# A one-core graph layer: tile widths of the last strips, one root, one comparison, and who makes the gate logits

## The chip, the cores and the metric

The kernel runs on one core of a Trainium2 chip. TensorE multiplies, VectorE, ScalarE and GpSimd (POOL) do elementwise work, and SyncE (SP) issues most DMAs. The metric is the device time of one execution in microseconds. The kernel before was timed three times: median 1168.58, from 1165.75 to 1169.1. One further execution was profiled.

## The reference

There are N = 3125 nodes with D = 256 features and E = 53125 weighted edges (src, dst), sorted by dst. In short:

```
xn = layernorm(x)
A[d, s] = sum of edge_weight over the edges s -> d      (3125 x 3125)
h  = A xn                                               (N x 256)
s0 = softmax((A h) W0^T + b0)                           (N x 128)
s1 = softmax((A [s0]) W1^T + b1)                        (N x 128)
gnn = tanh([s0, s1] + h)
mix = linear attention of xn: q, k, v projections, layernorm per head, k^T v, output projection
x1 = x + gnn + mix
probs = softmax(layernorm(x1) gate_w + gate_b)          (8 experts)
each token goes to its best expert if its place there is below the capacity of 489
out = x1 + (relu(token w1 + b1) w2 + b2) * prob
```

The reference runs four equal heads and averages them, and W1 enters as a 128 x 128 matrix.

## The kernel before

**Tiles, strips and units.** Nodes lie in 25 tiles of 128 (NT); the last tile holds 53 (LAST). The matrix A is built densely, one block of 128 sources by 128 destinations at a time. A strip is a group of destination tiles (STRIPS): six strips of four tiles (512 columns), and tile 24 alone (128 columns, of which 53 are nodes). A unit is one source tile j of one strip, so four blocks; the last strip has seven units of up to four source tiles. That makes 157 units (UNITS).

**The loop over units.** Every engine walks the same iterations, written out by hand with offsets. In iteration `it`, VectorE makes the one-hot operands of unit it-2 (`hots`, L1037 to L1046: source compared with a ramp, destination compared with a ramp, and, from unit 25 on, the source block times the edge weight). They lie in four buffers (`hot`). For the first 25 units (LEAD) ScalarE weighs them (`weigh`, L742). TensorE builds unit it-3 into one of two PSUM banks (`build`, L1491; an own-tile block, L1493, is added on the diagonal), ScalarE evicts it into the ring (`evac`, L752) and stores a chunk of five units to DRAM (`adj_dram`), and TensorE applies unit it-4 to xn (`apply`, L1508, last strip L1510), which accumulates h. At the end of a strip its h is copied out (`strip_out`), then every node tile is turned and multiplied by W0 (`hidden_node`, evicted by `hn_out`). The attention's products (`mix`, `mixed`) are placed in the loop at MIX_AT. The first 25 iterations also load and rank the edges (`spread`, `slot`, `ranks`, `slots`); the edge windows are loaded by SyncE one by one (L441 to L443). Four groups of windows are prepared on VectorE (`prepare`).

**The start.** ScalarE copies constants, waits for the centred k and v weights from TensorE and copies them (L687), and then takes the square root of the variances (`roots`, L698), on which the normalisation waits.

**The two z layers.** A is read back from DRAM, chunk by chunk, into a ring of five slots (L548). SyncE issues a load when the slot's old chunk is freed; the third load (slot 0) waits until the last unit is applied and all stores have landed. `strip(l, k)` multiplies by it (L1658), and other work is put between its 25 source tiles as inserts: `turns` (L1412 in layer 0, L1674 in layer 1), and in layer 1 also `gate_turn`, `logits` (L1694) and `counts` (L1703 to L1711). The second layer has its own strips (Z1): five of four tiles, then [20, 21], [22, 23] and [24]. [20, 21] and [22, 23] read the same five chunks.

**Gating.** After a strip of the second layer VectorE adds the bias (L1231), takes the maximum, normalises after ScalarE's exponentials, finishes x1 (L1247), takes moments (L1252, L1255) and an inverse root by iteration (`root`), places the group before (`slotted`), writes the normalised tokens (L1303), and for the first two tiles of each of four groups (DOTS = 4, DOT_TILES = 2) makes the eight gate logits itself, one fused multiply and sum each (`dots`, L1327). For the other tiles TensorE transposes x1 (`gate_turn`), ScalarE copies it (`xtout`) and TensorE multiplies by the gate (`logits`). `chosen` adds the bias and picks the expert; TensorE's `counts` waits for it. POOL scatters the tokens to DRAM. When all are there they are loaded back, and eight experts follow (L1746, L1758). Tiles 22 to 24 are one gating group.

A second path for inputs with too many edges per block (`more_rounds`) is not taken with these inputs.

Of the kernel before, what the change touches and what calls it, by code (L numbers as in the profile page):

```python
# [16 lines left out]
D = 256  # L17
# [46 lines left out]
DOTS, DOT_TILES = 4, 2  # L64
# [16 lines left out]

def chunk_of(u):
    return u // 5


def last_unit(n):
    return min(5 * n + 4, NU - 1)

# [8 lines left out]
for _t in range(NT - 1):  # L97
    _k, _i = _t // 4, _t % 4
    HN_AT[NT * _k + 30 + (5 * _i if _k < 5 else _i)] = _t
# [10 lines left out]
def graph_program(nc, a, out):  # L110
    ctx = ExitStack()
    with ctx:
# [320 lines left out]
        def _(sp):  # L433
# [42 lines left out]
            with more_rounds(sp):  # L476
# [11 lines left out]
                def put(c, jj, last):  # L488
# [4 lines left out]
                    to = adj_dram[31, :, jj * P:(jj + 1) * P] if last else adj_dram[30][:, ds(c * 5 * P + jj * P, P)]  # L493
                    sp.dma_start(to, e_tile[:, 6 * 512:NP]).then_inc(m_store, 16)
                    sp.wait_ge(m_store, j * 32 + 32)
                    sp.sem_inc(m_kept, 1)
                with sp.Fori(0, 4) as c:
                    for jj in range(5):
                        put(c, jj, False)
                for jj in range(5):  # L500
                    put(4, jj, True)
# [5 lines left out]
                sp.dma_start(e_chunk, adj_dram[30]).then_inc(m_chunk, 16)  # L507
                sp.wait_ge(m_app, 32)
                sp.dma_start(e_chunk[:, 0:5 * P], adj_dram[31, :, 0:5 * P]).then_inc(m_chunk, 16)
# [22 lines left out]
            for l in (0, 1):  # L532
                for q in range(NC):
# [13 lines left out]
                    w = 5 * 512 if q < NC - 1 else 5 * P  # L547
# [125 lines left out]
        def _(act):  # L673
# [71 lines left out]
            def evac(u):  # L745
                n = chunk_of(u)
                w = len(UNITS[u]) * P
                if u % 5 == 0 and n >= 2:
# [3 lines left out]
                nc.scalar.copy(RING[:, n % 2, u % 5 * 512:u % 5 * 512 + w], ps[:, u % 2, 0:w]).then_inc(s_bev, 1)  # L752
                if u == last_unit(n):
                    act.wait_ge(s_bev, u + 1)
                    w = 5 * 512 if n < NC - 1 else 5 * P
                    act.dma_start(adj_dram[n, :, 0:w], RING[:, n % 2, 0:w]).then_inc(s_ast[n % 2], 16)

            def strip_out(k):
                w = len(STRIPS[k]) * P
# [4 lines left out]
            roots(0)  # L764
            for j in range(3):
                normal(j)
# [30 lines left out]
            def zout(l, k):  # L797
                w = len((STRIPS, Z1)[l][k]) * P
# [20 lines left out]
            def xtout(k):  # L819
# [6 lines left out]
                for b in range(i0 // 2, (i0 + n + 1) // 2):  # L826
                    w = min(2, i0 + n - 2 * b)
                    last = nc.scalar.copy(xtb[g % 2][:, 2 * b:2 * b + w, :], ps[:, XTB + b, 0:w * D].rearrange("p (t n) -> p t n", n=D))
# [55 lines left out]
        def _(dve):  # L884
# [138 lines left out]
            def hots(u):  # L1023
# [7 lines left out]
                if u < NT * (NS - 1):  # L1031
                    field = lambda f: recs[:, f, j * NR + s:j * NR + s + n]
                else:
                    field = lambda f: recs[:, f, :].rearrange("p (t g) -> p t g", g=NR)[:, j:j + n, s]
                grid = lambda f: field(f).unsqueeze(2).to_broadcast([P, n, P])
                every = iota_n[:, :].unsqueeze(1).to_broadcast([P, n, P])
                v.tensor_tensor(h[:, 0, 0:n, :], every, grid(0), ALU.is_equal).then_inc(s_eq, 1)  # L1037
# [5 lines left out]
                last = v.tensor_tensor(h[:, 1, 0:n, :], every, grid(1), ALU.is_equal)  # L1043
                if u >= LEAD:
                    dve.wait_ge(s_eq, u + 1)
                    last = v.tensor_tensor(h[:, 0, 0:n, :], h[:, 0, 0:n, :], grid(2), ALU.mult)  # L1046
                last.then_inc(s_hot, 1)

            def strip_out(k):
                w = len(STRIPS[k]) * P  # L1050
# [113 lines left out]
            mixed(NT - 3)  # L1164
            hn_out(NT - 1)
# [622 lines left out]
```

## Time and profile before

| | |
|---|---|
| median of three executions | 1168.58 us |
| lowest and highest | 1165.75 and 1169.1 us |
| the profiled execution | 1178.36 us |
| its span | 1176.6 us |
| mean granted TensorE clock | 0.973 |
| TensorE busy | 1109.7 us (94%) |
| VectorE busy | 738.8 us (63%) |
| ScalarE busy | 315.3 us (27%) |

The span is the time from the first to the last recorded instruction, in one profiled execution. Busy time of TensorE is modelled from the starts of its instructions; an engine that isn't the bound may idle at no cost. The stages by time: up to about 226 us edges are ranked while the graph is built; from there to 622 the graph is built and applied; 626 to 767 is the first z layer; 767 to about 937 the second layer with the gating; 937 to the end the experts.

### The profile page before, as it was taken

To read this page: it belongs to the slowest core of one execution; us is meant where nothing else is said; L and a number is where in the kernel's file an instruction comes from. 1 tells how busy PE (TensorE), PEld (TensorE's weight loads), DVE (VectorE), ACT (ScalarE), POOL (GpSimd) and SP (SyncE) were. 2 spreads that over 40 slices of the span, in tenths; PEclk is the share of its full clock that TensorE was granted. 3 is DMA by queue.
4 is the path that set the end of the run, shared out by engine and by line. 5 is a ranking of instruction groups with operands and counts; after the bars stand their busy time and mean duration, and the time that the engine had idled before them with its cause. 6 is when DMAs were issued, how large, how long until landed. Compare 5 with 4: busy or idle time off the path is not lost.

```text
span 1176.6 us, 14070 instructions
## 1 busy us (share of the span) xinstructions
PE 1109.7 (94%) x4819; PEld 697.4 (59%) x4819; DVE 738.8 (63%) x1688; ACT 315.3 (27%) x1031; POOL 167.6 (14%) x206
## 2 busy tenths in 40 slices
PE   4879989999999999999998999999999699999995
PEld 2546666666666666666684444544448556666664
DVE  7989989998786977768740111116787425555444
ACT  4557767411212212112220110102112211112220
POOL 1013222301010100010000000000244421111111
PEclk8799989999999999999998999999999799999998
DMA  6110111123323333332228988797994475555620
GB/s 170 14 30 27 46 45 46 45 90 125 127 115 136 116 118 120 119 147 107 90 96 319 337 334 298 273 345 276 312 325 169 144 212 123 118 126 140 141 70 7
DMA packets 78869, 176.43 MB, mean 150 GB/s; under 512 B 33583, under 2 KB 62026, under 8 KB 66638
## 3 DMA queue, kind: packets, MB, share of 16 engines
q1 hardware_dynamic: 67550, 124.81, 33.3%
q10 hardware_dynamic: 7120, 42.67, 9.0%
q0 software_dynamic: 4128, 8.04, 2.0%
q8 instruction: 41, 0.67, 0.2%
q14 instruction: 30, 0.25, 0.1%
HBM read 114.87 MB, written 63.09 MB: 151 GB/s over the span
## 4 chain that ended last, share of the span: by engine, by line
PE 81%; DVE 8%; SPq 4%; issue 3%; ACT 2%; another core or an unknown queue 1%; DMA 0%; POOL 0%; POOLq 0%; DVEq 0%; ACTq 0%
PE ps L1508 20%; PE ps L1658 19%; PE ps L1491 11%; PE ps L1758 9%; PE ps L1746 9%; SPq L443 2%; PE ps L1534 2%; PE ps L1475 2%; PE ps L1461 1%; PE ps L1412 1%; PE ps L1761 1%; PE ps L1510 1%; DVE W L997 1%; SPq L441 1%
## 5 line engine op out<-in xcount | busy, mean ns | idle before, releaser
L1658 PE MATMUL ps<-RING,RY 128*128 128x512 f32 (+2 forms) x750 | 279.8, 531 | 4.4 <-issue 4.4
L1508 PE MATMUL ps<-RING,XX 128*128 128x512 f32 x600 | 282.6, 593 | 0.3 <-ACT RING L752 0.3
L1658 PEld LDWEIGHTS ps<-RING,RY 128*128 128x128 f32 x750 | 136.4, 196 | 131.0 <-issue 128.8
L1491 PEld LDWEIGHTS ps<-RING 128*128 128x128 f32 x1250 | 163.6, 193 | 45.8 <-issue 44.7
L752 ACT COPY RING<-ps 128x512 f32<-128x512 f32 (+1 forms) x157 | 91.8, 585 | 315.4 <-PE ps L1491 299.5
L1491 PE MATMUL ps<-RING 128*128 128x128 f32 x1250 | 170.8, 278 | 0.5 <-ACT RING L742 0.5
L1508 PEld LDWEIGHTS ps<-RING,XX 128*128 128x128 f32 x600 | 102.7, 191 | 72.9 <-issue 71.7
L1037 DVE TENSOR_TENSOR RING<-iota_n,RY 128x512 f32<-128x512 f32 (+1 forms) x157 | 108.1, 689 | 42.0 <-PE ps L1491 38.8
L1043 DVE TENSOR_TENSOR RING<-iota_n,RY 128x512 f32<-128x512 f32 (+1 forms) x157 | 117.4, 748 | 0.0
L1046 DVE TENSOR_TENSOR RING<-RING,RY 128x512 f32<-128x512 f32 x132 | 90.3, 684 | 0.0
L875 ACT ACTIVATE RY<-ps,b1T 128x489 f32<-128x489 f32 x64 | 42.9, 671 | 171.8 <-PE ps L1746 170.8
L1385 DVE SCALAR_TENSOR_TENSOR W<-ps,RING,W 128x256 f32<-128x256 f32 (+1 forms) x32 | 15.5, 484 | 98.8 <-PE ps L1758 97.8
L1216 DVE TENSOR_REDUCE nmx<-ps 128x4 f32<-128x512 f32 (+1 forms) x7 | 4.4, 635 | 113.6 <-PE ps L1412 113.6
L645 POOL DMA_INDIRECT xbuf_dram<-XX,sidx x25 | 25.1, 1002 | 341.4 <-DVE sidx L1315 335.9
L631 POOL TENSOR_TENSOR XX<-XX,bo_b 128x256 f32<-128x256 f32 x25 | 29.3, 1174 | 255.0 <-PE ps L1491 254.9
L668 POOL DMA_INDIRECT out<-W,RING x32 | 31.5, 985 | 188.9 <-DVE W L1392 152.0
L1758 PE MATMUL ps<-XT,RY 128*128 128x256 f32 (+1 forms) x256 | 55.9, 379 | 0.0
L1758 PE MATMUL ps<-RING,RY 128*128 128x256 f32 (+1 forms) x256 | 55.9, 379 | 0.0
L1475 PE MATMUL ps<-wkvT,XT 128*128 128x512 f32 x100 | 52.5, 651 | 3.5 <-ACT XT L715 3.5
L1746 PE MATMUL ps<-RING,XT 128*128 128x489 f32 x128 | 53.2, 574 | 0.0
L1746 PE MATMUL ps<-RING 128*128 128x489 f32 x128 | 53.1, 573 | 0.0
L1758 PEld LDWEIGHTS ps<-RING,RY 128*128 128x128 f32 (+1 forms) x256 | 47.4, 185 | 9.3 <-issue 1.8
(255 smaller groups left out, 1286.7 us busy)
## 6 DMA issues: line engine op xcount, KB each, us to landing
RING<-adj_dram SPq DMA_DIRECT2D x62, 1280.0 KB
adj_dram<-RING ACTq DMA_DIRECT2D x31, 1280.0 KB, 4.5
rbuf_dram<-W SPq DMA_DIRECT2D x8, 516.0 KB, 5.3
RING<-rbuf_dram SPq DMA_DIRECT2D x8, 516.0 KB, 4.1
xbuf_dram<-W SPq DMA_DIRECT2D x8, 512.0 KB, 3.3
XT<-in_L_ffn_w SPq DMA_DIRECT2D x16, 256.0 KB
XT<-in_L_ffn_w SPq DMA_DIRECT2D x4, 1024.0 KB
RING<-in_L_ffn_w SPq DMA_DIRECT2D x16, 256.0 KB
```

The source lines that it names most:

```text
L668: gp.indirect_dma_start(out[:, :], bass.IndirectOffsetOnAxis(ap=rbs[0:n, e % 2, c, D + 1:RES].bitcast(I32), axis=0), ybs[0:n, e % 2, c, :] ...
L752: nc.scalar.copy(RING[:, n % 2, u % 5 * 512:u % 5 * 512 + w], ps[:, u % 2, 0:w]).then_inc(s_bev, 1)
L875: nc.scalar.activation(hmT[:, f, 0:CAPX], ps[:, 2 + f % 3, 0:CAPX], ACT.Relu, bias=b1T[:, f, e:e + 1]).then_inc(s_hidv, 1)
L1037: v.tensor_tensor(h[:, 0, 0:n, :], every, grid(0), ALU.is_equal).then_inc(s_eq, 1)
L1043: last = v.tensor_tensor(h[:, 1, 0:n, :], every, grid(1), ALU.is_equal)
L1046: last = v.tensor_tensor(h[:, 0, 0:n, :], h[:, 0, 0:n, :], grid(2), ALU.mult)
L1475: last = nc.tensor.matmul(ps[:, PROD, :], XT[:, c, m * P:(m + 1) * P], wkvT[:, c, :], start=(c == 0), stop=(c == 1))
L1491: last = nc.tensor.matmul(o[:, i * P:(i + 1) * P], h[:, 0, i, :], h[:, 1, i, :], start=True, stop=(j != s))
L1508: last = nc.tensor.matmul(ps[:, ACC + dd, :], w, at, start=(j == 0), stop=True, skip_group_check=True)
L1658: last = nc.tensor.matmul(o, (Y if l == 0 else S0)[:, j, :], RING[:, slot_of[g % 5], i * across + first:i * across + first + w], start=(j ...
L1746: last = nc.tensor.matmul(ps[:, 2 + f % 3, 0:CAPX], w1s[s][:, c, f * P:(f + 1) * P], xbT[:, s, c, 0:CAPX], start=(c == 0), stop=(c == 1))
L1758: last = nc.tensor.matmul(o, hmT[:, f, c * P:c * P + n], w2s[s][:, f, :], start=(f == 0), stop=(f == 7))
```

## The change

It has four parts.

1. STRIPS becomes five strips of four tiles, [20, 21, 22] (384 columns) and [23, 24] (128 + 53 = 181 columns, ENDW). The units of the last strip take two source tiles and two destination tiles each: 13 units instead of 7, so 163 in all. Chunks 30 and 31 hold 14 and 11 source tiles of 181 columns (2534 and 1991 columns; before 2560 and 640); chunks of strip 5 are stored and loaded at their full 2560 columns, of which each unit fills 384 in 512. Products of tile 24 are 53 columns wide instead of 128. Node tile 23 is finished behind the loop, where before only tile 24 was. Z1 ends in [20, 21], [22] and [23, 24]; [20, 21] and [22] share their chunks.
2. ScalarE takes the first root before it copies the k and v weights.
3. For the first 25 units VectorE makes both comparisons in one instruction of 1024 elements. For the later ones the own-tile operands come first, then the two comparisons, then the product.
4. DOT_TILES = 3: VectorE makes the gate logits of three tiles in each of four groups.

```diff
-STRIPS = [list(range(4 * k, min(4 * k + 4, NT))) for k in range(7)]
+STRIPS = [list(range(4 * k, 4 * k + 4)) for k in range(5)] + [[20, 21, 22], [23, 24]]
-UNITS += [[(j, NT - 1) for j in range(i, min(i + 4, NT))] for i in range(0, NT, 4)]
+UNITS += [[(j, s) for j in range(i, min(i + 2, NT)) for s in STRIPS[-1]] for i in range(0, NT, 2)]
+ENDW = P + LAST
+ENDN = 14
-Z1 = STRIPS[:NS - 2] + [[20, 21], [22, 23], [24]]
+Z1 = STRIPS[:NS - 2] + [[20, 21], [22], [23, 24]]
-DOTS, DOT_TILES = 4, 2
+DOTS, DOT_TILES = 4, 3
...
+def width(tiles):
+    return sum(P if t < NT - 1 else LAST for t in tiles)
...
 def chunk_of(u):
-    return u // 5
+    return u // 5 if u < NT * (NS - 1) else NC - 2 + (u - NT * (NS - 1)) // (ENDN // 2)
...
+def chunk_width(n):
+    return 5 * 512 if n < NC - 2 else ENDW * (ENDN if n == NC - 2 else NT - ENDN)
...
-for _t in range(NT - 1):
+for _t in range(NT - 2):
...
-                    w = 5 * 512 if q < NC - 1 else 5 * P
+                    w = chunk_width(q)
                     sp.dma_start(RING[:, slot_of[g % 5], 0:w], adj_dram[q, :, 0:w]).then_inc(s_ald[g % 5], 16)
...
-            act.wait_ge(s_wt, 1)
-            for c in range(2):
-                nc.scalar.copy(wkvT[:, c, :], ps[:, 4 + c, :]).then_inc(s_wtc, 1)
...
             roots(0)
+            act.wait_ge(s_wt, 1)
+            for c in range(2):
+                nc.scalar.copy(wkvT[:, c, :], ps[:, 4 + c, :]).then_inc(s_wtc, 1)
...
             def evac(u):
-                w = len(UNITS[u]) * P
+                n, at = chunk_of(u), place_of(u)
+                w = width(s for _, s in UNITS[u])
...
 (hots, VectorE)
-                v.tensor_tensor(h[:, 0, 0:n, :], every, grid(0), ALU.is_equal).then_inc(s_eq, 1)
...
+                if u < LEAD:
+                    v.tensor_tensor(h[:, :, 0:n, :], iota_n[:, :].unsqueeze(1).unsqueeze(1).to_broadcast([P, 2, n, P]),
+                                    recs[:, 0:2, j * NR + s:j * NR + s + n].unsqueeze(3).to_broadcast([P, 2, n, P]), ALU.is_equal).then_inc(s_hot, 1)
+                    return
...
+                v.tensor_tensor(block(0), every, grid(0), ALU.is_equal).then_inc(s_eq, 1)
+                v.tensor_tensor(block(1), every, grid(1), ALU.is_equal)
+                dve.wait_ge(s_eq, u + 1 - LEAD)
+                v.tensor_tensor(block(0), block(0), grid(2), ALU.mult).then_inc(s_hot, 1)
...
 (build, TensorE)
-                    last = nc.tensor.matmul(o[:, i * P:(i + 1) * P], h[:, 0, i, :], h[:, 1, i, :], start=True, stop=(j != s))
+                    c = width(g for _, g in UNITS[u][:i])
+                    w = width([s])
+                    last = nc.tensor.matmul(o[:, c:c + w], h[:, 0, i, :], h[:, 1, i, 0:w], start=True, stop=(j != s))
...
 (apply, TensorE)
-                            last = nc.tensor.matmul(ps[:, ACC + dd, 0:P], w, at[:, i * P:(i + 1) * P], start=(j == 0), stop=True, skip_group_check=True)
+                        last = nc.tensor.matmul(ps[:, ACC + dd, 0:w], XN[:, j, dd * H:(dd + 1) * H], at[:, i * w:(i + 1) * w], start=(j == 0), stop=True, skip_group_check=True)
...
             mix(NT - 3)
+            hidden_node(NT - 2)
+            mix(NT - 2)
             hidden_node(NT - 1)
-            mix(NT - 2)
             mix(NT - 1)
...
 (strip, TensorE)
-                w = len(tiles) * P
+                w = width(tiles)
-                if tiles[0] == NT - 1:
-                    first, across, per = 0, P, 20
+                if tiles == STRIPS[-1]:
+                    first, across, per = 0, ENDW, ENDN
```

The path for further rounds is changed in the same way and isn't run.

## Rows read from the trace of the kernel before

**Rows 1.** The page: busy time, its share of the span, instructions; the chain by engine.

```profile
PE 1109.7 (94%) x4819; PEld 697.4 (59%) x4819; DVE 738.8 (63%) x1688; ACT 315.3 (27%) x1031; POOL 167.6 (14%) x206
...
PE 81%; DVE 8%; SPq 4%; issue 3%; ACT 2%; another core or an unknown queue 1%; DMA 0%; POOL 0%; POOLq 0%; DVEq 0%; ACTq 0%
```

**Rows 2.** Stages: length, busy PE, PEld, DVE, ACT, POOL, PE clock, DMA share, GB/s.

```profile
655.00:770.00 115.00, 113.83 (x322) 54.71 (x321) 19.07 (x36) 17.27 (x63) 0.00 (x0) 1.00 0.85 309
770.00:866.00 96.00, 96.00 (x280) 46.48 (x279) 56.89 (x241) 11.62 (x37) 16.77 (x16) 1.00 0.88 315
866.00:937.00 71.00, 59.48 (x293) 45.59 (x292) 47.24 (x214) 15.12 (x48) 25.80 (x26) 0.91 0.55 182
```

**Rows 3.** The chain in order of time (start, us, what): TensorE's prices.

```profile
595.14 1.72 PE ps L1508 x4
596.86 0.89 PE ps L1491 x8
...
606.60 1.79 PE ps L1510 x16
...
701.39 21.46 PE ps L1658 x50
...
857.96 0.44 PE ps L1412 x4
...
861.83 0.79 PE ps L1694 x8
```

**Rows 4.** Timeline of TensorE, second layer (start, us, line, operation, idle before).

```profile
841.29 1.05 PE L1674 MATMUL ps<-W1T,W 128*128 128x128 f32 x8
...
865.14 1.05 PE L1674 MATMUL ps<-W1T,W 128*128 128x128 f32 x8
...
917.46 0.90 PE L1674 MATMUL ps<-W1T,W 128*128 128x128 f32 x4 [4.05 <-issue]
...
920.14 5.97 PE L1658 MATMUL ps<-RING,RY 128*128 128x128 f32 x32
```

**Rows 5.** Timeline of VectorE, second layer.

```profile
794.92 0.69 DVE L1231 TENSOR_TENSOR W<-ps,gb_b 128x512 f32<-128x512 f32 x1 [10.47 <-PE ps L1674]
...
806.50 0.43 DVE L1327 SCALAR_TENSOR_TENSOR XT<-XX,RY 128x256 f32<-128x256 f32 x1
...
815.04 0.17 DVE L1278 TENSOR_TENSOR wkvT<-wkvT,gate_b 128x16 f32<-128x16 f32 x1 [1.09 <-PE ps L1694]
...
866.23 0.69 DVE L1231 TENSOR_TENSOR W<-ps,gb_b 128x512 f32<-128x512 f32 x1 [1.14 <-PE ps L1674]
...
889.50 0.69 DVE L1231 TENSOR_TENSOR W<-ps,gb_b 128x512 f32<-128x512 f32 x1 [0.79 <-remote]
...
902.01 0.42 DVE L1231 TENSOR_TENSOR W<-ps,gb_b 128x256 f32<-128x256 f32 x1
...
922.73 0.42 DVE L1231 TENSOR_TENSOR W<-ps,gb_b 128x256 f32<-128x256 f32 x1 [9.28 <-remote]
...
929.40 0.29 DVE L1231 TENSOR_TENSOR W<-ps,gb_b 128x128 f32<-128x128 f32 x1
```

**Rows 6.** The chain in order of time, first 220 us.

```profile
59.41 1.64 DMA HB<-in_edge_weight
...
141.71 0.69 DVE RING L1037
```

**Rows 7.** TensorE's waits: who for whom, us in total, times, longest.

```profile
PE ps L1461 <- DVE W L997: 9.8, 7, 1.8
```

**Rows 8.** Timeline of VectorE, two comparisons of the ranking stage.

```profile
152.25 0.68 DVE L1037 TENSOR_TENSOR RING<-iota_n,RY 128x512 f32<-128x512 f32 x1
152.85 0.69 DVE L1043 TENSOR_TENSOR RING<-iota_n,RY 128x512 f32<-128x512 f32 x1
```

**Rows 9.** Timeline of TensorE, start of the first z layer.

```profile
626.11 6.16 PE L1658 MATMUL ps<-RING,RY 128*128 128x512 f32 x8 [4.42 <-issue]
```

**Rows 10.** The DMA view, issues: line, engine, count, KB each, us to landing.

```profile
adj_dram<-RING ACTq DMA_DIRECT2D x1, 320.0 KB, 9.3
```

More of the change, by code:

```diff
@@ L492, in put @@
                                  e_tile[:, 0:6 * 512].rearrange("p (k n) -> p k n", k=6)).then_inc(m_store, 16)
-                    to = adj_dram[31, :, jj * P:(jj + 1) * P] if last else adj_dram[30][:, ds(c * 5 * P + jj * P, P)]
-                    sp.dma_start(to, e_tile[:, 6 * 512:NP]).then_inc(m_store, 16)
+                    if last:
+                        to = adj_dram[30 + j // ENDN, :, j % ENDN * ENDW:(j % ENDN + 1) * ENDW]
+                    else:
+                        to = adj_dram[30][:, ds(c * 5 * ENDW + jj * ENDW, ENDW)]
+                    sp.dma_start(to, e_tile[:, STRIPS[-1][0] * P:STRIPS[-1][0] * P + ENDW]).then_inc(m_store, 16)
                     sp.wait_ge(m_store, j * 32 + 32)
                     sp.sem_inc(m_kept, 1)
-                with sp.Fori(0, 4) as c:
+                with sp.Fori(0, 2) as c:
                     for jj in range(5):
                         put(c, jj, False)
-                for jj in range(5):
-                    put(4, jj, True)
+                for c in range(2, 5):
+                    for jj in range(5):
+                        put(c, jj, True)
                 with sp.Fori(0, 6) as k:
@@ L1490, in build @@
                 for i, (j, s) in enumerate(UNITS[u]):
-                    last = nc.tensor.matmul(o[:, i * P:(i + 1) * P], h[:, 0, i, :], h[:, 1, i, :], start=True, stop=(j != s))
+                    c = width(g for _, g in UNITS[u][:i])
+                    w = width([s])
+                    last = nc.tensor.matmul(o[:, c:c + w], h[:, 0, i, :], h[:, 1, i, 0:w], start=True, stop=(j != s))
                     if j == s:
-                        last = nc.tensor.matmul(o[:, i * P:(i + 1) * P], h[:, 0, 4, :], h[:, 1, 4, :], start=False, stop=True)
+                        last = nc.tensor.matmul(o[:, c:c + w], h[:, 0, 4, :], h[:, 1, 4, 0:w], start=False, stop=True)
                 last.then_inc(s_bmm, 1)
@@ L1606, in _, with rows @@
                 pe.wait_ge(m_add, NT + 1)
-                def rows(w, tiles, loaded):
+                def rows(w, tiles, loaded, across=512, first=0):
                     pe.wait_ge(m_chunk, loaded)
@@ L1611, in rows @@
                         for dd in range(2):
-                            last = nc.tensor.matmul(ps[:, ACC + dd, 0:w], XN[:, j, dd * H:(dd + 1) * H], e_chunk[:, i * w:(i + 1) * w],
+                            last = nc.tensor.matmul(ps[:, ACC + dd, 0:w], XN[:, j, dd * H:(dd + 1) * H], e_chunk[:, i * across + first:i * across + first + w],
                                                     start=(j == 0), stop=True, skip_group_check=True)
@@ L1649, in strip @@
                     i = j % per
-                    g = l * NC + 5 * (tiles[0] // 4) + j // per
+                    g = l * NC + 5 * strip_with(tiles[0]) + j // per
                     if i == 0 and not again:
```

73 lines of the change are left out of this document (36 added, 37 removed).

## The prediction, made before the result was known

> **What bounds the kernel now.** I read the page first. TensorE is busy 94% of the span and holds 81% of the chain of waits, VectorE 8% [rows 1]. The table by stage, read next, shows where that stops: from 655 to 770 TensorE is busy 113.8 of 115 us, from 770 to 866 all of it, and from 866 to 937 only 59.5 of 71, while VectorE works 57 of 96 and 47 of 71 us [rows 2]. So columns taken from TensorE count fully up to about 866; behind that one must ask for VectorE. Then the chain in order of time gave the prices of TensorE's work [rows 3], the timelines of TensorE and VectorE the periods of the second graph layer and its end [rows 4, 5], and chain, waits and timeline the first 220 us [rows 6 to 8].
>
> **1. The root first.** ScalarE's root waits behind two copies of weights (1.1 us). But the chain at 59.41 is SyncE's long list of window loads, issued one by one, which ends in a landing [rows 6]. What starts earlier waits longer for that landing, and so does the first k and v product, whose weight copies now stand behind the root and its wait for VectorE's variances: 0. If that cover were gone, 1.1 us at most.
>
> **2. Comparisons in one.** In 25 units one comparison of 1024 takes the place of two of 512. Their starts are 0.60 us apart [rows 8]; L1231 takes 0.69 for 512 columns and 0.29 for 128 [rows 5], so 384 columns cost 0.40, 512 cost 0.53, and some 0.07 of the 0.60 is the fixed part that one comparison saves, an estimate. TensorE is the chain for most of this stage; VectorE stands on it around 141.71 and three more times, each time with one such pair, and TensorE waited for its L997 9.8 us in all [rows 6, 7]. Four times 0.07: -0.3. Bounds: 0, and 25 x 0.07 = -1.7. In the later units only the order changes: the product now waits behind a comparison that it doesn't need, and both were ahead of it before: 0.
>
> **3. Columns 384 and 181, building the graph.** Prices per instruction (a float32 product is two): 512 columns 1.72/4 = 0.430, 128 columns 1.79/16 = 0.112, built blocks 0.89/8 = 0.111 [rows 3]. The line through the first two gives 0.324 at 384 columns and 0.156 at 181.
> Strip 5: 100 apply instructions save 0.106 each, 10.6; 25 blocks fewer are built, 50 x 0.111 = 5.6. Together -16.2.
> Last strip: before, 50 x 0.111 + 100 x 0.112 = 16.8. After, 25 full blocks 5.6, 25 blocks of 53 columns, 100 apply instructions x 0.156 = 15.6. A block of 53 columns isn't in the trace. The row of 8 columns is 0.79/8 = 0.099 [rows 3], so 53 cost between that and 0.111; below 0.099 only if the 8-column row is slow for another reason, at least 53/128 x 0.111 = 0.046. I take 0.099, since 53 is nearer to 8: 5.0. Sum 26.2, +9.4.
> Net **-6.8**; the ends are -6.2 and -9.5.
> The rows say that short products don't go below 0.099 us. The Trainium skill (TensorE: Matmul & The Clock Gate, the clock-gate part) says that a matmul takes its columns by the clock plus some 2.5 ns, with a floor of about 25 ns. By that page the 50 instructions would cost 50 x 0.05 = 2.5 us, not 5.0, and the sum would be 2.5 us lower; no row here shows a short float32 product that fast.
> Hidden: the six extra units add six evictions on ScalarE, which is mostly idle here, and 18 VectorE operations. In the last strip VectorE needs 3 x 0.60 = 1.8 us a unit [rows 8] against TensorE's 8 x 0.105 + 8 x 0.156 = 2.1, so it keeps up; without the four-deep buffer of comparisons it would cost 13 x 0.3 = 4 us at most. Node 23 moves behind the loop: same work, one more handover between two mixes of 0.9 us.
>
> **4. The change of stage.** The first load into the third buffer waits for the last store of the graph; TensorE idles 4.42 us before 626.11, and that store of 320 KB takes 9.3 us to land [rows 9, 10]. It grows to 991 KB. 0.69 MB more at 309/0.85 = 364 GB/s [rows 2] is 1.9 us. TensorE needs that buffer only 15 tiles (13 us) later, but its idle time is unexplained ("issue") and falls into the same burst of DMA. Ends 0 and +1.9; I take **+0.9**.
>
> **5. First z layer.** 50 x 0.106 less 50 x 0.044 = **-3.1**; the wait for ScalarE after the short strip also gets shorter, some -0.5. Chunks are still 1.31 MB for strip 5 but TensorE now eats one in 3.2 us, and at 364 GB/s a load needs 3.6. Five loads fall 1.8 us behind; the ring is four chunks ahead, so it is hidden. With that cover gone: +1.8.
> So the second layer's first strip ends 0.3 + 6.8 + 3.1 + 0.5 - 0.9 = **9.8 us earlier**.
>
> **6. Three tiles on VectorE.** This is where it is decided. Sixteen dots take from 806.50 to 813.95 (815.04 less 1.09 idle), 0.466 each. VectorE's loop from 866.23 to 889.50 is 23.27, of which 0.79 idle: 22.5 of its own. TensorE's strip is 865.14 - 841.29 = 23.85 [rows 4, 5]. Balanced today. The third tile adds 8 x 0.466 = 3.7 to VectorE, takes one 0.1 away, and takes from TensorE half of 0.44 + 0.79, 0.6 [rows 3]. Then VectorE needs 26.1 and TensorE 23.2: **VectorE bounds the loop.** Its first period (no slots to place yet) is 25.0. From the start at 794.92: 25.0 + 3 x 26.1 = 103.3, so what began at 889.50 begins at 898.2, 8.7 later before the 9.8 are taken off. TensorE will stand about 10 us in the strip of tiles 20 and 21, at its counts, which wait for this.
>
> **7. The end.** In the old clock: the next two blocks take 12.5 (902.01 - 889.50) and 11.4 as before, so tile 22's begins at 922.1, where 22 and 23 began at 922.73. Before, VectorE idled 9.28 us ahead of that [rows 5]: the delay vanishes in it. Tile 22's block is shorter, but TensorE still owes 20 tiles x 2 x 0.156 = 6.2 plus 1.4 for logits and turning: 7.6 against 6.67 (929.40 - 922.73). In the last block some ten operations grow from 128 to 256 columns or from one to two; L1231 goes from 0.29 to 0.42 [rows 5]: +1.5. Sum: -0.6 + 0.9 + 1.5 = **+1.8**. The experts' part is untouched. Tile 22's strip lasts only 5.6 us, less than the load of its successor's chunk (issue, 3.6 us), but TensorE stands there for VectorE anyway.
>
> **The sum and which time it is against.** Against the profiled execution (1178.36; span 1176.6 and 1.8 around it): 1178.4 - 9.8 + 1.8 = 1170.4. But that execution is 9.8 us above the median, 1168.58. And it has a hole that nothing in the trace explains: 4.05 us of idle "issue" on TensorE before 917.46 [rows 4], then VectorE resumes 4.6 us after that turn has ended, 9.28 "remote" [rows 5]. Together 8.7, about the surplus. I take it that ordinary runs don't have it. Then before reaches tile 22's block at 914, VectorE has no idle time there, and the delay of step 6 isn't absorbed: 8.7 + 1.8 - 9.8 = +0.7, **1169 us**. What the columns give, the third tile takes.
>
> **Rivals.**
> *The hole is in every run of before.* Then step 6 costs nothing: 1168.6 - 9.8 + 1.8 = **1160.6**. For it: it is in the trace, near scatters and loads. Against: its size equals the surplus of this one execution.
> *TensorE's low clock at the end (slower).* The 10 us stand of step 6 is new. After the 4.05 us one the clock fell, and 32 short products took 5.97 us, 0.187 instead of 0.112 [rows 4]. If it is still low when tiles 22 to 24 run (about 80 instructions at 0.11 to 0.16), they take some 5 us more, and this time VectorE waits for them: **1174**. It decides if TensorE's wait for VectorE's choice of tiles 16 to 19 exceeds some 3 us just ahead. For it: that second wait is 3 us by my count. Against: between the two it works 10 us nearly without a gap.
> The Trainium skill (TensorE: Matmul & The Clock Gate, the part on the clock gate) says the slow clock is the default and sustained work releases it; the trace agrees, and 32 instructions at 0.187 are its price here.
> *The third tile is hidden.* If VectorE could keep below 23.2, by taking up its 2.4 us of waits for ScalarE per loop, only the columns are left, and TensorE's 0.6 x 4: **1155**. Against: the engine runs in order, 22.5 + 3.6 contains those waits.
>
> **Chances.** Forecast 0.42, around it +-3; hole in every run 0.26; low clock 0.24; hidden 0.08. 0.3% of 1168.58 is 3.5 us, about what a measurement of this kernel tells from no change: below 1165.1 is faster, above 1172.1 slower. The forecast's own spread gives 0.02 and 0.04 to the sides. Faster 0.36, same 0.36, slower 0.28. Range 1159 to 1175; the forecast's own is 1166 to 1172.
>
> **What would show it.** Steps 3 and 5: VectorE's first L1231 of the second layer (794.92, [rows 5]) comes 9 to 11 us earlier; last-strip apply instructions of 181 columns at 0.156; built blocks of 53 at 0.099. Step 4: TensorE's idle before the z stage 4.4 to 6.3. Step 6: L1231 of the z1 loop 26.1 apart, with no idle before it; TensorE idle about 10 us at L1703, waiting for VectorE. Step 7: VectorE idle under 1 us before tile 22's block. Wrong if the period stays at 23.8, if the apply instructions at 181 cost as much as 256, or if VectorE idles again for 9 us at the end.

## The result, and the profile after

The changed kernel takes 1172.75 us (median of 7 runs, 1170.26 to 1175.16), the kernel before in the same session 1168.56 (7 runs). The ratio is 1.0041, 95% interval 1.0029 to 1.0054: 4.2 us slower by the medians (4.8 by the ratio), where 1169 was predicted, with 1166 to 1172 as the forecast's own range and 1159 to 1175 as the range over all rivals.

The page of the changed kernel, busy time and the chain by engine (for [rows 1]), and then the table by stage (for [rows 2]; columns: window, length, busy PE, PEld, DVE, ACT, POOL, PE clock, DMA share, GB/s):

```profile
PE 1093.5 (93%) x4795; PEld 697.3 (60%) x4795; DVE 750.4 (64%) x1741; ACT 313.6 (27%) x1038; POOL 169.0 (14%) x206
...
PE 73%; DVE 15%; issue 4%; SPq 4%; ACT 3%; DMA 1%; POOLq 0%; POOL 0%; ACTq 0%; DVEq 0%
```

```profile
770.00:866.00 96.00, 96.00 (x270) 45.53 (x269) 68.87 (x291) 12.62 (x45) 17.16 (x16) 1.00 0.88 316
866.00:937.00 71.00, 51.53 (x263) 41.60 (x262) 49.93 (x233) 13.26 (x41) 29.02 (x30) 0.81 0.48 162
```

TensorE's busy time fell by 16 us (by 12 against the profile of experiment 1), and VectorE's share of the chain went from 8% to 15%. Look at the last window: TensorE is busy 51.5 us of 71 where it was 59.5, at a granted clock of 0.81 where it was 0.91 (65.1 and 0.93 in experiment 1). VectorE's timeline in the second layer, the bias add that begins each block (start, us, line, operation, idle before; for [rows 5]):

```profile
784.88 0.69 DVE L1261 TENSOR_TENSOR W<-ps,gb_b 128x512 f32<-128x512 f32 x1 [10.47 <-PE ps L1703]
809.93 0.69 DVE L1261 TENSOR_TENSOR W<-ps,gb_b 128x512 f32<-128x512 f32 x1
836.11 0.69 DVE L1261 TENSOR_TENSOR W<-ps,gb_b 128x512 f32<-128x512 f32 x1
...
862.27 0.69 DVE L1261 TENSOR_TENSOR W<-ps,gb_b 128x512 f32<-128x512 f32 x1
888.39 0.69 DVE L1261 TENSOR_TENSOR W<-ps,gb_b 128x512 f32<-128x512 f32 x1
900.89 0.42 DVE L1261 TENSOR_TENSOR W<-ps,gb_b 128x256 f32<-128x256 f32 x1
913.46 0.29 DVE L1261 TENSOR_TENSOR W<-ps,gb_b 128x128 f32<-128x128 f32 x1 [1.72 <-PE ps L1703]
921.99 0.42 DVE L1261 TENSOR_TENSOR W<-ps,gb_b 128x256 f32<-128x256 f32 x1 [1.45 <-PE ps L1703]
```

The blocks of the loop are 25.05, 26.18, 26.16 and 26.12 us apart, and no block of the loop behind the first waits for TensorE any more. TensorE's timeline, for [rows 9] and [rows 4]: the start of the first layer, then the two places where it now stands for VectorE:

```profile
620.10 20.19 PE L1687 MATMUL ps<-RING,RY 128*128 128x512 f32 x41 [5.77 <-issue]
...
888.46 0.21 PE L1732 MATMUL ps<-wkvT,upto_b 128*128 128x32 bf16 x1 [9.36 <-DVEq L1322]
...
906.08 0.21 PE L1732 MATMUL ps<-wkvT,upto_b 128*128 128x32 bf16 x1 [3.73 <-DVEq L1322]
...
906.18 3.76 PE L1687 MATMUL ps<-RING,RY 128*128 128x128 f32 x16
...
913.04 0.38 PE L1703 MATMUL ps<-W1T,W 128*128 128x128 f32 x2
...
914.38 5.17 PE L1687 MATMUL ps<-RING,RY 128*128 128x181 f32 x32
...
921.24 0.71 PE L1703 MATMUL ps<-W1T,W 128*128 128x128 f32 x4 [0.40 <-ACT W L829]
```

The two L1703 are the turns that let VectorE's last two blocks begin, 8.20 us apart. The table by stage for three short stretches behind the second stand (columns as above) has the granted clock at 0.50, the lower of its two levels (1.2 GHz), then a mix of both, and 1.00 when the last strip runs:

```profile
906.00:910.00 4.00, 3.92 (x21) 3.92 (x22) 3.47 (x18) 0.00 (x0) 3.08 (x4) 0.50 0.44 166
910.00:913.00 3.00, 3.00 (x18) 3.00 (x17) 1.61 (x8) 0.85 (x2) 1.21 (x3) 0.74 0.08 29
914.00:919.00 5.00, 5.00 (x35) 5.00 (x35) 2.89 (x15) 1.02 (x4) 3.89 (x4) 1.00 0.20 72
```

The DMA view's issues, for [rows 10]; the last store of the graph is three times as large and takes 12.0 us to land:

```profile
adj_dram<-RING ACTq DMA_DIRECT2D x1, 995.5 KB, 12.0
```

### The profile page after: what moved, and what is told of

It is laid out like the page before. It is cut to its first block, busy times and chain, and to the rows that moved or that the text cites. A ratio compares the mean times of both kernels' runs of the same rounds, so it can differ in the third digit from the quotient of the medians.

```text
span 1171.0 us, 14088 instructions
## 1 busy us (share of the span) xinstructions
PE 1093.5 (93%) x4795; PEld 697.3 (60%) x4795; DVE 750.4 (64%) x1741; ACT 313.6 (27%) x1038; POOL 169.0 (14%) x206
## 4 chain that ended last, share of the span: by engine, by line
PE 73%; DVE 15%; issue 4%; SPq 4%; ACT 3%; DMA 1%; POOLq 0%; POOL 0%; ACTq 0%; DVEq 0%
PE ps L1538 20%; PE ps L1687 15%; PE ps L1523 11%; PE ps L1787 9%; PE ps L1775 9%; DVE XT L1357 4%; SPq L465 2%; PE ps L1562 2%; PE ps L1505 2%; PE ps L1491 1%; PE ps L1442 1%; DVE W L1022 1%; ACT W L836 1%; SPq L463 1%; DVE bst L1282 1%
## 5 line engine op out<-in xcount | busy, mean ns | idle before, releaser
L1538 PE MATMUL ps<-RING,XX 128*128 128x512 f32 (+2 forms) x700 | 291.9, 542 | 1.0 <-DVE W L1082 1.0
L1687 PE MATMUL ps<-RING,RY 128*128 128x512 f32 (+4 forms) x750 | 275.8, 526 | 5.8 <-issue 5.8
L774 ACT COPY RING<-ps 128x512 f32<-128x512 f32 (+3 forms) x163 | 91.2, 560 | 311.5 <-PE ps L1523 297.5
L1523 PE MATMUL ps<-RING 128*128 128x128 f32 (+1 forms) x1250 | 170.2, 276 | 0.1
L1538 PEld LDWEIGHTS ps<-RING,XX 128*128 128x128 f32 x700 | 118.5, 192 | 68.8 <-issue 60.7
L1073 DVE TENSOR_TENSOR RING<-iota_n,RY 128x512 f32<-128x512 f32 (+1 forms) x138 | 91.2, 661 | 34.5 <-PE ps L1523 31.8
L1074 DVE TENSOR_TENSOR RING<-iota_n,RY 128x512 f32<-128x512 f32 (+1 forms) x138 | 100.5, 728 | 0.0
L1076 DVE TENSOR_TENSOR RING<-RING,RY 128x512 f32<-128x512 f32 (+1 forms) x138 | 91.1, 660 | 0.0
L1246 DVE TENSOR_REDUCE nmx<-ps 128x4 f32<-128x512 f32 (+2 forms) x7 | 4.4, 634 | 111.9 <-PE ps L1442 111.9
```

The source lines that it names most:

```text
L774: nc.scalar.copy(RING[:, n % 2, at:at + w], ps[:, u % 2, 0:w]).then_inc(s_bev, 1)
L1073: v.tensor_tensor(block(0), every, grid(0), ALU.is_equal).then_inc(s_eq, 1)
L1074: v.tensor_tensor(block(1), every, grid(1), ALU.is_equal)
L1076: v.tensor_tensor(block(0), block(0), grid(2), ALU.mult).then_inc(s_hot, 1)
L1523: last = nc.tensor.matmul(o[:, c:c + w], h[:, 0, i, :], h[:, 1, i, 0:w], start=True, stop=(j != s))
L1538: last = nc.tensor.matmul(ps[:, ACC + dd, 0:w], XN[:, j, dd * H:(dd + 1) * H], at[:, i * w:(i + 1) * w], start=(j == 0), stop=True, skip_g ...
```

## The experiments

Each was timed beside runs of the kernel before on the same chip. The quoted expectations call a kernel by the name in its heading.

### 1. The kernel before, profiled again

No edit. The prediction rested on a hole of some 9 us in the one profile of before that there was.

> The kernel before, unchanged, profiled once more. Theory (the hole is in one execution only): the profiled time is 1166 to 1171 us, VectorE's first bias add of the second layer is near 794.9 us after the span's start, the one of tiles 22 and 23 comes 46 to 48 us after that of tiles 16 to 19's predecessor rather than 56, and VectorE's idle ahead of it is below 2 us, with no idle of 4 us on TensorE ahead of its preceding turn. Rival (the hole is in every execution): VectorE idles 9 us again ahead of that bias add, TensorE 4 us, and the profiled time is about 1178 us, or 1168 with the surplus somewhere else.

Profiled time 1168.23, span 1166.5. VectorE's timeline, for [rows 5]:

```profile
794.31 0.69 DVE L1231 TENSOR_TENSOR W<-ps,gb_b 128x512 f32<-128x512 f32 x1 [9.85 <-PE ps L1674]
...
888.14 0.69 DVE L1231 TENSOR_TENSOR W<-ps,gb_b 128x512 f32<-128x512 f32 x1
900.64 0.42 DVE L1231 TENSOR_TENSOR W<-ps,gb_b 128x256 f32<-128x256 f32 x1
912.52 0.42 DVE L1231 TENSOR_TENSOR W<-ps,gb_b 128x256 f32<-128x256 f32 x1 [1.02 <-PE ps L1674]
919.29 0.29 DVE L1231 TENSOR_TENSOR W<-ps,gb_b 128x128 f32<-128x128 f32 x1 [0.19 <-PE ps L1674]
```

The block of tiles 22 and 23 waits 1.02 us, not 9.28. The second layer begins 0.6 us from where it did, and the block of tiles 22 and 23 10.2 us earlier. None of the eleven profiles that follow has the hole either, nor has that of the changed kernel. What made it in that one execution stays open; it belonged to the execution and not to the kernel. From here on this profile is what after is compared with.

### 2. The third tile alone

```diff
-DOTS, DOT_TILES = 4, 2
+DOTS, DOT_TILES = 4, 3
```

and ScalarE's `xtout` copies tile by tile as in the change.

> The kernel before with three tiles of gate logits on VectorE in place of two, nothing else. Theory (VectorE becomes the bound of the second layer): the bias adds of VectorE in that loop come 26 us apart in place of 23.8, TensorE stands about 10 us at the counts of the strip of tiles 20 and 21, and the time is 8 to 11 us above before, 1177 to 1180 us, ratio 1.007 to 1.0095. Rival (the hole of 9 us at the end is in every execution and takes the delay up): within 1.5 us of before. Rival (the third tile is hidden in VectorE's waits): 2 us below before.

1177.93 against 1168.21; ratio 1.0080 (1.0065 to 1.0094): +9.7 us. VectorE's timeline:

```profile
795.03 0.69 DVE L1231 TENSOR_TENSOR W<-ps,gb_b 128x512 f32<-128x512 f32 x1 [9.98 <-PE ps L1674]
...
872.38 0.69 DVE L1231 TENSOR_TENSOR W<-ps,gb_b 128x512 f32<-128x512 f32 x1
898.51 0.69 DVE L1231 TENSOR_TENSOR W<-ps,gb_b 128x512 f32<-128x512 f32 x1
```

26.13 us apart. From the first block to the fifth it is 103.48, where experiment 1 has 93.83: +9.65, the whole loss. The theory stands; the hole in every run and the hidden third tile fall.

### 3. Columns only (the third tile taken back)

```diff
 (the changed kernel)
-DOTS, DOT_TILES = 4, 3
+DOTS, DOT_TILES = 4, 2
```

> The changed kernel with two tiles of gate logits on VectorE, so columns, root and comparisons changed and the gating as before. Theory: the second layer starts 9.8 to 10 us earlier than in before and nothing is given back but 1 to 2 us at the end; 1159 to 1161 us, ratio 0.992 to 0.9935, about 12 to 13 us below the changed kernel; TensorE works through from the layer's start to the strip of tiles 20 and 21. Rival (the third tile costs little, and the columns gain little because time comes back at the stage change or in the last strips): 1166 to 1171 us. Low clock: with no stand of TensorE at the counts the granted clock of the last 70 us stays above 0.9 and the last strip's 64 instructions of 181 columns cost 0.157 each; if the slow products after the 3.7 us stand were from something other than that stand, the four-tile products of 128 columns take 0.22 each here too.

1161.66 against 1168.21; ratio 0.9946 (0.9929 to 0.9962): -6.55 us. That is between the theory (1159 to 1161) and its rival (1166 to 1171). The second layer begins 10.46 us earlier than in experiment 1, so the columns gain what was predicted; then 3.9 us come back: 1.5 up to the last block (from the first block to it 126.49 in place of 124.98) and 2.4 behind it, from there to the experts' first product (21.88 in place of 19.51). The next fence is TensorE's timeline there: its last stand for VectorE and, 14.2 us later, the turn that lets the last block begin. In experiment 1 the two are 12.9 us apart (905.83 to 918.77).

```profile
895.37 0.19 PE L1732 MATMUL ps<-wkvT,upto_b 128*128 128x32 bf16 x1 [3.79 <-DVEq L1322]
...
909.59 0.71 PE L1703 MATMUL ps<-W1T,W 128*128 128x128 f32 x4 [0.40 <-ACT W L829]
```

Tile 22's strip is so short that TensorE reaches the counts of tiles 16 to 19 before VectorE has them: it stands 3.79 us with two tiles too, and the wider last strip is still ahead of it. My text missed this: it said that TensorE would work through, and it had the low clock down as a thing of the third tile. The 16 products of 128 columns behind the stand take 3.07 us here (895.46 to 898.53), 0.19 each.

The same kernel's TensorE timeline in the graph gives the prices (differences of starts; an operation's own time overlaps the next):

```profile
575.37 1.46 PE L1538 MATMUL ps<-RING,XX 128*128 128x384 f32 x4
576.66 0.83 PE L1523 MATMUL ps<-RING 128*128 128x128 f32 x6
...
583.01 0.99 PE L1523 MATMUL ps<-RING 128*128 128x128 f32 x8
583.84 1.46 PE L1538 MATMUL ps<-RING,XX 128*128 128x181 f32 x8
585.13 0.38 PE L1442 MATMUL ps<-ident,W 128*128 128x128 f32 x2
...
589.46 0.41 PE L1442 MATMUL ps<-ident,W 128*128 128x128 f32 x2 [1.37 <-DVE RY L1087]
```

384 columns: 1.29/4 = 0.323 (predicted 0.324). 181 columns: 1.29/8 = 0.161 (0.156). Two full and two 53-column blocks: 0.83; less 4 x 0.111 it leaves 0.097 per instruction of 53 columns (0.099). The last row is a stand of 1.37 us that nobody had predicted: VectorE comes from the wait for the strip's end and still has units of 1.8 us each to do when TensorE wants to turn the next node tile (its release is L1087, VectorE's copy of the node tile before).

### 4. Start only (root and comparisons)

```diff
 (the kernel before, ScalarE)
-            act.wait_ge(s_wt, 1)
-            ... the two weight copies
             roots(0)
+            act.wait_ge(s_wt, 1)
+            ... the two weight copies
 (VectorE, hots: the body of the changed kernel for u < LEAD, and its order of the later units)
```

> The kernel before with the root ahead of the weight copies, one comparison of 1024 elements in the first 25 units, and the later units' own-tile operands first; columns and gating as before. Theory: within 0.5 us of before at either side, 0.3 us expected, since the start is set by the landing of the edge windows and TensorE is the chain after it. Rival (VectorE sets the ranking stage): 25 times 0.07, 1.7 us below before. Rival (the changed order in the 125 later units costs, because the product stands right behind the comparison): 1 to 3 us above before.

1166.24 against 1168.21; ratio 0.9984 (0.9975 to 0.9993): -2.0 us, more than the theory had.

### 5. Counts later

```diff
 (columns only, TensorE)
-            strip(1, kb, {3: [later(turns, 1, ka)], 4: [later(logits, ka - 1)], 14: [later(counts, ka - 1)], 22: [later(gate_turn, ka)]})
+            strip(1, kb, {3: [later(turns, 1, ka)], 4: [later(logits, ka - 1)], 24: [later(counts, ka - 1), later(gate_turn, ka)]})
```

> Columns only, and in the strip of tile 22 TensorE's counts of tiles 16 to 19 and its turning of tiles 20 and 21 stand behind the strip's last product in place of behind its 15th and 23rd. Theory (in columns only, TensorE stands 3.8 us at those counts for VectorE, and the 14 us of work that it still has behind them then set when the last two tiles begin): TensorE's stand shrinks to 1.3 us or less, tile 22's block on VectorE starts 0.8 us earlier, that of tiles 23 and 24 some 3 to 4 us earlier, and the time is 3 to 4 us below columns only, 1158 us, ratio 0.991 to 0.992. Rival (VectorE's own work or the loads of the last chunks set the end): within 1 us of columns only.

TensorE's timeline, the same two instructions as in experiment 3:

```profile
897.22 0.19 PE L1732 MATMUL ps<-wkvT,upto_b 128*128 128x32 bf16 x1 [1.56 <-DVEq L1322]
...
907.97 0.71 PE L1703 MATMUL ps<-W1T,W 128*128 128x128 f32 x4 [0.40 <-ACT W L829]
```

They are 10.8 us apart in place of 14.2, and the last block on VectorE begins 123.0 us after the layer's first block (785.71 to 908.72) in place of 126.5: 3.5 us, as the theory said. The median says less: 1160.64 against 1168.46, ratio 0.9935 (0.9921 to 0.9948), 1.0 us below columns only (1.3 by the ratios), in intervals that are each 3 us wide, where 3 to 4 us were expected. In the profile the second layer began 1.9 us later than in columns only, which is spread of the earlier stages. In the two later kernels that hold this edit (9 and 10) the same distance is 124.6 us, for a reason given under experiment 9. So the mechanism is shown in the trace, by 1.9 to 3.5 us; in the time it is 1.0 to 1.3 us and not clear of the spread.

### 6. The stands filled

```diff
 (the changed kernel, TensorE; nobody reads the products)
+            def busy(n):
+                for _ in range(n):
+                    nc.tensor.matmul(ps[:, XTB, :], ident[:, :], S0[:, 0:4, :], start=True, stop=True)
 (strip ka)  15: [later(busy, 10), later(counts, ka - 2)]
 (strip kb)  14: [later(busy, 4), later(counts, ka - 1)]
```

> The changed kernel, with 10 products of 512 columns that nobody reads ahead of TensorE's counts in the strip of tiles 20 and 21, and 4 ahead of those in the strip of tile 22, so that its stands of 9.4 and 3.7 us are mostly filled. Theory (the low clock that follows the stands costs some 1 to 2 us at the end): the granted clock from 866 to 937 us is above 0.95 in place of 0.81, the 16 products of 128 columns behind the second counts take some 0.12 each in place of 0.22, tile 22's block on VectorE begins 1 to 1.5 us earlier, and the time is 1 to 2 us below the changed kernel. Rival (the clock costs nothing since VectorE bounds): the same time as the changed kernel within 0.5 us. Rival (the clock is the main part of the loss, 5 us as in the prediction): 1168 us.

TensorE's timeline:

```profile
878.75 8.75 PE L1750 MATMUL ps<-RY,ident 128*128 128x512 f32 x20
888.25 0.19 PE L1732 MATMUL ps<-wkvT,upto_b 128*128 128x32 bf16 x1 [0.75 <-DVEq L1322]
...
903.58 3.60 PE L1750 MATMUL ps<-RY,ident 128*128 128x512 f32 x8
...
907.09 2.03 PE L1687 MATMUL ps<-RING,RY 128*128 128x128 f32 x16
```

The 16 products behind the second counts take 1.87 us to the next start (907.09 to 908.96), in the changed kernel 3.55 (906.18 to 909.73). Tile 22's block begins 23.63 us after that of tiles 16 to 19, in the changed kernel 25.07: 1.44 less. The granted clock from 907 to 911 is 1.00 in place of 0.50. The time is 1171.53 against 1168.46, ratio 1.0026 (1.0015 to 1.0037): 1.2 us below the changed kernel by the medians, 1.8 by the ratios, whose intervals overlap. The clock's price is therefore taken from the trace. It is 1.4 us at least, neither nothing nor 5; since the unread products end 0.9 us later than the old stand (counts at 907.01 in place of 906.08), a little more is possible, up to the 1.72 us that VectorE stood ahead of tile 22's block in the changed kernel (0.27 here). One number missed: the mean clock of the window rose to 0.88, not 0.95, since a gap of 2.9 us at 894 us, with a granted clock of 0.57 in the 4 us behind it, and the wait at the end stay.

### 7 and 8. Root alone, comparisons alone

The edits of experiment 4, one each.

> The kernel before with the root taken ahead of the weight copies, nothing else. Theory (start_only's gain of 2.0 us is VectorE's, in the ranking stage): 0 within 0.5 us. Rival (the root is on the start's path): 1.0 to 2.0 us below before, and TensorE's first normalised tile is turned 1 us earlier.

> The kernel before with the one comparison of 1024 elements in the first 25 units and the later units' own-tile operands first, nothing else. Theory: 1.5 to 2 us below before, since VectorE saves 0.07 us in each of 25 units and sets the ranking stage. Rival: within 0.5 us of before, as the prediction had it.

Root: 1167.93 against 1168.46, ratio 0.9999 (0.9988 to 1.0010). Comparisons: 1167.75, ratio 0.9994 (0.9985 to 1.0003). For the root no effect is seen, within 1.2 us either way; the comparisons are worth 0 to 1.7 us.

### 9. Store split

```diff
 (counts later; node tiles 20 to 22 three units apart)
-    HN_AT[NT * _k + 30 + (5 * _i if _k < 5 else _i)] = _t
+    HN_AT[NT * _k + 30 + (5 * _i if _k < 5 else 3 * _i)] = _t
 (ScalarE, evac: of the last chunk, the first three units are stored as soon as they are there; the waits for all stores count 16 more)
+                if u == first_unit(NC - 1) + HALF - 1:
+                    act.wait_ge(s_bev, u + 1)
+                    act.dma_start(adj_dram[n, :, 0:half], RING[:, n % 2, 0:half]).then_inc(s_ast[n % 2], 16)
```

> Counts later, with two edits in the graph's end. The node tiles 20 to 22 are turned three units apart in place of one; theory: the 1.37 us stand of TensorE near 589 us goes, since VectorE has by then caught up with the 1.8 us units it owes; rival: it is only moved. And the last chunk is stored in two parts, the first three units (6 source tiles of 181 columns) as soon as they are there; theory of the prediction (the size of the last store adds 0.9 us to TensorE's idle ahead of the first z layer): the idle goes from 5.2 to 5.8 us back to about 4.4 us; rival (the size has no part in it): 5.0 us or more. Time 1157 to 1159 us.

1158.99 against 1167.21, ratio 0.9924 (0.9911 to 0.9937). The stand at 589 us is gone and not moved (no idle of TensorE over 0.5 us from 578 to the end of the graph). The idle ahead of the first layer is not smaller but 5.90 us, though the last store is now 452 KB:

```profile
620.58 19.82 PE L1692 MATMUL ps<-RING,RY 128*128 128x512 f32 x41 [5.90 <-issue]
```

So the size of the last store is not what TensorE waits for: the mechanism of the prediction's step 4 falls.

This profile also shows why the last block comes 124.6 us after the first and not 123.0 as in experiment 5. TensorE's timeline behind the same counts:

```profile
896.53 0.19 PE L1737 MATMUL ps<-wkvT,upto_b 128*128 128x32 bf16 x1 [1.58 <-DVEq L1327]
...
897.43 3.02 PE L1692 MATMUL ps<-RING,RY 128*128 128x181 f32 x10
```

The stand is as long as in experiment 5 (1.58 and 1.56 us), but the 10 products behind it take 2.82 us to the next start, at a granted clock of 0.51, where there they take 1.55 at 1.00. Experiment 10 is like this one (a stand of 1.57, then 0.53). So one and the same short stand leaves the clock high in one execution and low in another, and that is 1.6 us here.

### 10. Loads later

```diff
 (as store split, the last chunk stored in one again; SyncE)
                     elif g == 1:
                         sp.wait_ge(s_bmm, NU)
+                        sp.wait_ge(s_hrd, NT)
```

> As store_split, with the last chunk stored in one again, and SyncE issues the second and third load of the first z layer only when the last node tile is out (some 6 us later). Theory (TensorE's idle ahead of the first z layer is something of its own that has to come through the burst of DMA of one store and two loads, which fills all engines at that time): the idle falls from 5.2 to 5.8 us to 3 us or less, and the time by 1 to 2.5 us unless TensorE then waits for the later loads. Rival (the idle is a fixed 4.4 us plus the size of the store): unchanged, and the time the same or longer.

1155.07 against 1167.21; ratio 0.9897 (0.9882 to 0.9912), 3.9 us below store split: the fastest version of the study, 12.1 us below before, where the changed kernel is 4.2 above it. Two edits part it from store split, and the unsplit store was not timed by itself; experiment 11 has the loads alone. TensorE's timeline, then the table by stretches of 2 us around its idle time (columns as above):

```profile
614.88 1.52 PE L1688 MATMUL ps<-RING,RY 128*128 128x512 f32 x3 [2.79 <-issue]
```

```profile
610.00:612.00 2.00, 2.00 (x12) 1.32 (x11) 1.26 (x5) 0.00 (x0) 0.00 (x0) 1.00 0.00 0
612.00:614.00 2.00, 0.09 (x1) 0.00 (x0) 0.42 (x1) 0.00 (x0) 0.00 (x0) 1.00 0.60 146
614.00:616.00 2.00, 1.12 (x3) 0.67 (x4) 0.00 (x0) 0.00 (x0) 0.00 (x0) 1.00 0.99 410
```

The DMA engines stand still when TensorE comes to the end of the graph. What the engine itself asks for can be seen in the queues. The DMA view by queue (packets, MB, share of 16 engines) of columns only from 617 to 618 us, 2.3 to 3.3 us into TensorE's idle time, and of loads later from 612 to 613, where its idle time has just begun:

```profile
q1 hardware_dynamic: 20, 0.20, 48.1%
q10 hardware_dynamic: 25, 0.20, 47.0%
q8 instruction: 1, 0.02, 6.0%
```

```profile
q1 hardware_dynamic: 4, 0.04, 21.2%
q8 instruction: 1, 0.02, 6.5%
```

One packet on a queue of the kind "instruction" lands in both. Narrowed to a quarter of a microsecond it is at 617.25 to 617.5 and at 612.25 to 612.5, and TensorE starts at 619.92 and 614.88. The kept traces have each packet's own start and duration (0.96 to 1.29 us for this one). In all fourteen of them TensorE starts 2.5 to 2.8 us behind the packet's start, and 1.52 to 1.55 us behind its end. The packets of the other instruction queue (q14) have no such distance: in experiments 10 and 11 the next one comes only when TensorE has started again. The packet begins 1.9 to 2.2 us after the last product in seven profiles with the old columns, 2.7 to 3.8 us after it in five with the new ones, and 0.2 us after it here (in experiment 11 0.9 us before it). So TensorE seems to wait for a fetch of code here, and under the burst of loads it comes late. That the queue is TensorE's is an inference from these times, since the view names no engine; and that the fetch is due to the branch over the path that isn't run is argued from the place in the code, no kernel without that branch was run. The Trainium skill (Runtime: NRT & Kernel Launch, the part on instruction fetch) says that each sequencer fetches its code itself in blocks of 16 KiB over a DMA queue, and that a branch out of the fetched pages has to wait for one. The packet's 0.02 MB and TensorE's wait for it agree with that.

The clock holds as well: in the first 4 us of the layer it is 1.00 and the products take 0.44 us each (7.53 for 17); in columns only, where the engine had stood for 5.17 us, it is 0.63 and they take 0.72 (4.30 for 6).

### 11. Loads later in the kernel before

The edit of experiment 10 in the kernel before, nothing else.

> The kernel before, with SyncE's second and third load of the first z layer issued only when the last node tile is out; nothing else. Theory (the idle ahead of the first z layer belongs to the loads' burst, not to this change): TensorE's idle goes from 4.4 us to about 2.8 us and the granted clock behind it stays higher, so 2 to 3.5 us below before, ratio 0.997 to 0.998. Rival (only the larger last store of the changed kernel made the burst costly): within 0.5 us of before.

1165.67 against 1169.23, ratio 0.9966 (0.9952 to 0.9979): -3.6 us. TensorE's idle time is 1.94 us in place of 4.4, and the packet is on its way before it begins. The clock did not hold here: it is 0.62 in the layer's first 4 us, behind 1.94 us of idle, where in experiment 10 it was 1.00 behind 2.79. The cost is the old kernel's; the change only adds to it (some 1.1 us of idle).

### 12. Root and comparisons once more

The kernel of experiment 4.

> Start only once more, since its 2.0 us below before are more than the sum of its parts measured alone (0.1 and 0.7 us). Theory (the parts add, and the difference is spread of the measurement): 0.3 to 1.3 us below before. Rival (the two help only together, since the earlier root lets VectorE's saved time count): 2 us below before again.

1167.93 against 1169.23, ratio 0.9990 (0.9979 to 1.0002): -1.3 us. With experiments 4, 7 and 8 everything is consistent with 1 to 2 us for both together. Whether they help each other is not settled; it would be under a microsecond.

## Why the prediction was right

The place and the mechanism were right: the columns give about 10 us up to the second layer, and the third tile takes them away again, because VectorE becomes the bound. The time was 3.8 us too low: inside the stated range, just outside the forecast's own (1166 to 1172), and nearer to the rival of the low clock (1174), though the clock made only 1.4 us of it. The kernel came out slower, to which 0.28 had been given. The terms, in profiles, changed kernel against experiment 1:

| step | predicted | measured | from |
|---|---|---|---|
| 1 to 5: start of the second layer | -9.8 | -9.4 | 794.31 to 784.88; the mean of five kernels with the columns against three without: -9.9 |
| 6: first to fifth block | +8.7 | +9.7 | 93.83 to 103.51 |
| 7: on to tile 22's block | -0.6 | +0.7 | 24.38 to 25.07 |
| 7: on to the last block | +0.9 | +1.8 | 6.77 to 8.53 |
| 7: on to the experts' first output products | +1.5 | +1.8 | 32.70 to 34.52 |
| sum | +0.7 | +4.5 | spans 1166.5 to 1171.0 |

**Steps 1 and 2** (-0.3): too small, 1 to 2 us by experiments 4 and 12. The chain's four passages were counted, while VectorE's 25 savings probably also shorten waits that the chain doesn't pass; that is not shown.

**Steps 3 and 5**: prices within some 3%. An instruction of 53 columns takes 0.097 us. The prediction's estimate from the floor of about 25 ns that the Trainium skill gives (TensorE: Matmul & The Clock Gate, the clock-gate part) was 0.05; the measurement decides. The stand of 1.37 us at the change of strips was missed: a four-deep buffer hid VectorE's rate, but not that `hn_out` comes behind several units of it. The first layer got 4.2 us shorter (means 168.8 to 164.6) where 3.6 were predicted.

**Step 4** (+0.9): size about right (4.4 to 4.7 us of idle in seven profiles without the columns, 5.2 to 6.3 in five with them: +1.1 in the mean), cause wrong. It isn't the size of the last store but a fetch of code that comes late under two loads of 1.3 MB, by experiments 9 to 11.

**Step 6**: VectorE's own time per loop was right to 0.1 us (26.1). The term was 1.0 too small because it was taken against a block that had been 0.79 us late by the hole's profile [rows 5], which experiment 1 doesn't have.

**Step 7** holds most of the error, in three terms (1.3, 0.9 and 0.3). On to tile 22's block: with the stands filled it is 23.63 - 24.38 = -0.75, near the predicted -0.6; the other 1.4 us are the low clock. That was the rival with 0.24, at the right place and with the right condition (the second stand was 3.73 us), but with 1.4 us and not 5, because the last strip's products of 181 columns ran at 0.157 each again: the clock was back before them. VectorE's idle time ahead of tile 22's block, which was to stay under 1 us, is 1.72. On to the last block: the 7.6 us of TensorE's work from tile 22's block on were right (40 instructions at 0.157, 1.4 for counts, logits and turning). What was left out is the wait for ScalarE's copy ahead of the last turn (0.40, with the handover some 0.5), which makes the turns 8.20 us apart, and that the last turn now has two tiles, so that VectorE begins 0.75 us behind its start where it was 0.42: 8.53 in all, and the same 8.53 with the stands filled. When both blocks begin is set by TensorE's work from the counts of tiles 16 to 19 on, 14 to 15 us, all behind a wait for VectorE; experiment 5 shortened that. The last term, on to the experts, was 1.8 where 1.5 was predicted.

**The hole** was rightly left out, on the ground of its size alone. By the prediction's own terms the kernel would have been faster, had it been in every run.

**Slips without effect.** The rival of the hidden third tile adds up to 1156.4 (1168.6 - 9.8 - 2.4), not 1155. And the 5.6 us of tile 22's strip are more than the 3.6 of a load, not less.

## What to carry to other kernels

Where two engines are near balance in a loop (here VectorE with 22.5 us of its own in TensorE's 23.85), work that is moved from one to the other is hidden only as far as the slack goes: of the 3.7 us moved, 2.3 were paid in every turn. Take the price from the period of the engine that receives the work. When a stage gets shorter on one engine, look again at where it waits for another inside the stage: a wait placed behind the strip's 15th source tile cost 0.7 us before and is now 3.7 us in front of the critical work; moving it 10 source tiles on took 1.9 to 3.5 us off the trace, where the new columns had lost 1.5. And where an idle time marked "issue" ends a fixed time behind a packet on an instruction queue, leave the DMA engines free ahead of it: holding two loads back by 4 to 6 us was worth 3.6 us in the kernel before and 3.9 in store split (there together with the unsplit store), for one line of code.

## What the runs showed of the hardware that was not expected

- A profile of a single execution can hold a hole of 9 us in the middle of a stage. Its distance from the median said so.
- TensorE's restart at the change of stage comes 1.52 to 1.55 us behind the end of one packet on an instruction queue, in fourteen of fourteen profiles. Under a burst of loads that packet begins 1.9 to 3.8 us after the last product, with the loads held back between 0.9 us before it and 0.2 us after it.
- A float32 product of 53 columns with new weights costs 0.097 us per instruction, one of 8 columns 0.099, one of 128 columns 0.111: below 128 columns little is gained.
- After a stand of 3.7 us TensorE ran 16 products of 128 columns at 0.22 us each, twice the usual, at a granted clock of 0.50, and the last strip right behind at 1.00; with the stand filled by unread products they cost 0.12.
- The length of a short stand alone doesn't say what the clock does behind it: 1.00 behind 1.56 us (experiment 5) and behind 2.79 (10), 0.51 behind 1.58 (9), 0.62 behind 1.94 (11), 0.57 behind 2.92 (6). The prediction's "some 3 us" is no sharp limit.
